# A state-space scan layer on eight cores: batched start statistics, five weight casts on another engine, a scan ring of four

## The reference, cut

```python
xn = layernorm(x)                                   # x: (1, 16384, 1024)
delta = softplus(einsum('btd,ed->bte', xn, Wd) + bd)
a_pos = softplus(a_log) + 0.0001                    # (1024, 16)
# for every token t, channel d and state n (16 states):
#   state = exp(-delta*a_pos)*state + delta*b_param*xn
# y = sum of the 16 states
attn = einsum('btd,ed->bte', y, Wo) + bo
real = einsum('bti,io->bto', xn, cos(theta + theta_noise))
imag = einsum('bti,io->bto', xn, sin(phi + phi_noise))
out  = x + attn + sqrt(real*real + imag*imag)
```

## Time and profile before

| | us |
|---|---|
| median of 2 runs | 1109.86 (1109.3 to 1110.43) |
| the profiled execution's own time | 1110.03 |
| its span on the slowest core (core 4) | 1108.2 |
| spans of the eight cores | 1099.7 to 1108.2 |
| first scan starts on core 4 | 71.09 |

### The profile page before, as it was taken

The page is one execution under the profiler, slowest core; times in us unless marked ns, Lnnn a source line. Parts: engine busy times, 40 slices in busy tenths (PEclk is TensorE's granted clock), DMA queues, the critical chain, the costliest instruction groups (busy, mean ns, idle before and its releaser), DMA issues.

```text
span 1108.2 us, 9244 instructions; the slowest of 8 cores (1099.7 to 1108.2 us)
## 1 busy us (share of the span) xinstructions
PE 572.1 (52%) x2239; PEld 240.3 (22%) x2248; DVE 816.4 (74%) x725; ACT 582.4 (53%) x927; POOL 150.4 (14%) x132
## 2 busy tenths in 40 slices
PE   0522444445457554556545456665555555454785
PEld 0300111112113231222211113343222211121343
DVE  3449888898853349999999993334899999999423
ACT  4485876666633226666665553332466655555430
POOL 2467000000011200000000001121000000000232
PEclk9985555556678866666665668887766556666799
DMA  8887101000011410000000001331100000000023
GB/s 235 208 224 195 57 29 29 29 19 1 0 48 57 122 37 0 1 1 0 1 1 1 0 0 48 88 114 58 43 1 1 0 1 1 1 0 1 29 72 114
DMA packets 36324, 51.65 MB, mean 47 GB/s; under 512 B 3120, under 2 KB 19760, under 8 KB 36272
## 3 DMA queue, kind: packets, MB, share of 16 engines
q1 hardware_dynamic: 33584, 42.68, 13.8%
q0 software_dynamic: 2688, 8.39, 2.3%
HBM read 42.67 MB, written 8.39 MB: 46 GB/s over the span
## 4 chain that ended last, share of the span: by engine, by line
DVE 46%; PE 17%; ACT 17%; issue 17%; DMA 2%; DVEq 1%; ACTq 0%; POOL 0%; SPq 0%; POOLq 0%
DVE grot L723 36%; ACT abar L677 9%; PE pd L852 6%; ACT bdg_bf L171 3%; PE pt L570 3%; PE pt L580 2%; DVE sfm L866 2%; DVE vbuf L333 2%; DMA xsub<-xin 2%; DVE gcar L734 1%; PE pd L278 1%; PE pe L357 1%; PE py L880 1%; DVE xsub L419 1%; PE pt L357 1%
## 5 line engine op out<-in xcount | busy, mean ns | idle before, releaser
L723 DVE TENSOR_TENSOR_SCAN grot<-abar,gcar,vbuf 128x768 bf16<-128x768 f32 (+1 forms) x384 | 647.0, 1742 | 41.1 <-ACT abar L677 32.4
L677 ACT ACTIVATE abar<-delta,nega 128x768 f32<-128x768 f32 (+1 forms) x384 | 341.2, 898 | 242.5 <-DVE grot L723 240.3
L767 PE MATMUL pe<-grot,bdg_bf 128*128 128x384 bf16 x256 | 86.6, 443 | 119.1 <-DVE grot L723 119.1
L767 PE MATMUL py<-grot,bdg_bf 128*128 128x384 bf16 x256 | 85.7, 441 | 119.7 <-DVE grot L723 119.6
L278 PE MATMUL pd<-xnbf,wd_bf 128*128 128x384 bf16 (+1 forms) x368 | 98.7, 450 | 18.1 <-ACT xsub L297 14.7
L754 PE MATMUL py<-grot,bdg_bf 128*128 128x512 bf16 x61 | 32.5, 544 | 78.9 <-DVE grot L723 78.5
L852 PE MATMUL pd<-ybf,wo_bf 128*128 128x384 bf16 (+1 forms) x318 | 72.4, 377 | 0.3 <-issue 0.2
L620 POOL TENSOR_TENSOR xsub<-r,i 128x384 f32<-128x384 f32 (+1 forms) x9 | 18.1, 2009 | 388.4 <-ACT i L612 388.4
L570 PE MATMUL pt<-xnbf,cos_bf 128*128 128x384 bf16 (+1 forms) x319 | 69.9, 367 | 0.2 <-issue 0.2
L754 PE MATMUL pe<-grot,bdg_bf 128*128 128x512 bf16 x63 | 33.7, 545 | 68.5 <-DVE grot L723 68.5
L278 PEld LDWEIGHTS pd<-xnbf,wd_bf 128*128 128x128 bf16 x368 | 49.6, 135 | 67.2 <-issue 58.9
(11 more groups left out here) (105 smaller groups left out, 559.3 us busy)
## 6 DMA issues: line engine op xcount, KB each, us to landing
xsub<-xin SPq DMA_DIRECT2D x14, 512.0 KB, 4.4
xres<-xin SPq DMA_DIRECT2D x32, 192.0 KB, 2.5
out<-osub POOLq DMA_DIRECT2D x32, 192.0 KB, 2.7
xres<-xin SPq DMA_DIRECT2D x8, 256.0 KB, 4.1
out<-osub POOLq DMA_DIRECT2D x8, 256.0 KB, 3.4
r<-wdt SPq DMA_DIRECT2D x6, 256.0 KB, 5.4
i<-wdt SPq DMA_DIRECT2D x6, 256.0 KB, 6.0
etmp<-tht SPq DMA_DIRECT2D x6, 256.0 KB, 4.9
```

The costliest lines, as they stand in the source:

```text
L677: sx = run("scalar", lambda e, sl=sl_ab, par=par, dt=dt, n=n, tp=tp: e.activation(out=abar[:, sl * TP:sl * TP + tp], in_=delta[:, par * TP ...
L723: vs = run("vector", lambda e, g=gsl, sl=sl_ab, par=par, dt=dt, n=n, tp=tp: e.tensor_tensor_scan(out=grot[:, g * TP:g * TP + tp], data0=ab ...
L767: td = run("tensor", lambda e, c=c, g=gsl, dt=dt, n=n, bb=ypair[c]: e.matmul(bb[:, 0:384], bdg_bf[:, (dt * NST + n) * P:(dt * NST + n + 1) ...
```

## The change

Three edits.

1. In stage A of phase 0 the five tiles get their own scratch columns (`bn6` grows to 12 columns a tile, `bnA` holds mean and variance of all, `lnv` has six columns). DVE does the statistics of all five tiles without waiting for ACT, and then one Ln, one Exp and one product handle all five.
2. The last five of the 16 Wd pieces (11 to 15) no longer use the staging slots and POOL. SP loads them into five idle places (`vbuf`, `osub`, `xres`) without a wait, and ACT casts them after stage A, ahead of the diagonals of blocks 2 to 5. The Wd product waits for both engines' casts.
3. The ring `grot` has four slots in place of five, and the carried columns are copied after n = 3, 7, 11 and 15, four at a time.

```diff
-        grot = sbuf("grot", [P, 5 * TP], BF16)
+        grot = sbuf("grot", [P, 4 * TP], BF16)
...
+        wds_slots = [vbuf[:, 0:512], vbuf[:, 512:1024], osub[:, 512:1024],
+                     xres[:, 0:512], xres[:, 512:1024]]
+        wds_sems = ["LX5", "LW0", "LW1", "LR", "LR1"]
...
             if kind == "cast":
+                piece = off // 512
+                if piece >= 11:
+                    q = piece - 11
+                    la = run("sync", lambda e, s=src0, q=q: e.dma_start(
+                        out=wds_slots[q], in_=s), wds_sems[q], 16)
+                    wd_s_jobs.append((q, la, dst, off))
+                    continue
                 sl = wslot_next()
...
-                for ts in range(NSUBL[0]):
+                nsub0 = NSUBL[0]
+                vag = 0
+                for ts in range(nsub0):
                     wait("vector", xsems[ts], lxev[ts])
-                    wait("vector", "V", prev_vts)
                     run("vector", lambda e, ts=ts, a=xslots[ts]: e.bn_stats(
-                        out=bn6[:, 0:6], in_=a[:, 0:512]), "V")
+                        out=bn6[:, ts * 12:ts * 12 + 6], in_=a[:, 0:512]), "V")
...
                     wait("vector", "V", vst)
-                    wait("vector", "S", prev_s1)
-                    vag = run("vector", lambda e: e.bn_aggr(out=bn2[:], in_=bn6[:]), "V")
...
+                    vag = run("vector", lambda e, ts=ts: e.bn_aggr(
+                        out=bnA[:, ts * 2:ts * 2 + 2],
+                        in_=bn6[:, ts * 12:ts * 12 + 12]), "V")
...
+                s1 = run("scalar", lambda e, a=var_ap, w=nsub0: e.activation(
+                    out=lnv[:, 0:w], in_=a, func=AF.Ln, bias=cvals[:, 1:2]), "S")
+                wait("scalar", "S", s1)
+                s2 = run("scalar", lambda e, w=nsub0: e.activation(
+                    out=rstd6[:, 0:w], in_=lnv[:, 0:w], func=AF.Exp,
+                    scale=-0.5), "S")
+                wait("vector", "S", s2)
+                v1 = run("vector", lambda e, a=mean_ap, w=nsub0: e.scalar_tensor_tensor(
+                    out=negmr6[:, 0:w], in0=a, scalar=cvals[:, 2:3],
+                    in1=rstd6[:, 0:w], op0=ALU.mult, op1=ALU.mult), "V")
...
                 emit_stage_a(0)
+                for (q_, la_, dst_, off_) in wd_s_jobs:
+                    wait("scalar", wds_sems[q_], la_)
+                    s_ev = run("scalar", lambda e, d=dst_, o=off_, q=q_: e.activation(
+                        out=d[:, o:o + 512], in_=wds_slots[q], func=AF.Copy), "S")
...
                 for dtq in range(2, 6):
                     bdg_ev[dtq] = ("S", emit_diag_s(dtq, 0, NST))
...
-                    gsl = n % 5
+                    gsl = n % 4
...
-                    if n in (4, 9, 14):
-                        g0 = n - 4
+                    if n % 4 == 3:
+                        g0 = n - 3
                         wait("vector", "V", vs)
-                        gs = grot[:].rearrange("q (s t) -> q s t", s=5)[:, :, tp - 1:tp]
+                        gs = grot[:].rearrange("q (s t) -> q s t", s=4)[:, :, tp - 1:tp]
                         vc = run("vector", lambda e, a=gs, dt=dt, g0=g0: e.tensor_copy(
-                            out=gcar[:, dt * NST + g0:dt * NST + g0 + 5], in_=a), "V")
...
-                    elif n == 15:
```

More of the change, by code:

```diff
@@ L80, in _build @@
         cvals = sbuf("cvals", [P, 3])
-        bn6 = sbuf("bn6", [P, 12])
+        bn6 = sbuf("bn6", [P, 12 * NSUB])
         bn2 = sbuf("bn2", [P, 2])
-        lnv = sbuf("lnv", [P, 1])
+        bnA = sbuf("bnA", [P, 2 * NSUB])
+        lnv = sbuf("lnv", [P, NSUB])
         rstd = sbuf("rstd", [P, 1])
@@ L241, in _build @@
         ev_abar_free = [0, 0, 0]
-        ev_g_free_t = [0, 0, 0, 0, 0]
-        ev_g_free_v = [("V", 0)] * 5
+        ev_g_free_t = [0, 0, 0, 0]
+        ev_g_free_v = [("V", 0)] * 4
         ev_sfm_free_t = [0, 0]
@@ L274, in emit_sp_mm @@
                 wait("tensor", "V", bfree_v.get(keys[c], 0))
-                wait("tensor", "G", grp_done[id(wd_bf)])
+                gdw = grp_done[id(wd_bf)]
+                if isinstance(gdw, list):
+                    for sm_, evv_ in gdw:
+                        wait("tensor", sm_, evv_)
+                else:
+                    wait("tensor", "G", gdw)
                 tmm = None
@@ L329, in emit_vmult @@
                 wait(eng, "T", ev_p0_slots.get(5, 0))
+            if p == 0 and dt < 2:
+                wait(eng, "S", ev_wds_s[0])
             for rj in (8, 9, 10):
@@ L404, in emit_a_subtile @@
             wait("vector", "S", prev_s1)
-            vag = run("vector", lambda e: e.bn_aggr(out=bn2[:], in_=bn6[:]), "V")
+            vag = run("vector", lambda e: e.bn_aggr(out=bn2[:], in_=bn6[:, 0:12]), "V")
             wait("scalar", "V", vag)
@@ L409, in emit_a_subtile @@
             s1 = run("scalar", lambda e: e.activation(
-                out=lnv[:], in_=bn2[:, 1:2], func=AF.Ln, bias=cvals[:, 1:2]), "S")
+                out=lnv[:, 0:1], in_=bn2[:, 1:2], func=AF.Ln, bias=cvals[:, 1:2]), "S")
             wait("scalar", "S", s1)
             s2 = run("scalar", lambda e: e.activation(
-                out=rstd[:], in_=lnv[:], func=AF.Exp, scale=-0.5), "S")
+                out=rstd[:], in_=lnv[:, 0:1], func=AF.Exp, scale=-0.5), "S")
             wait("vector", "S", s2)
@@ L441, in emit_stage_a @@
                     vst = run("vector", lambda e, ts=ts, a=xslots[ts]: e.bn_stats(
-                        out=bn6[:, 6:12], in_=a[:, 512:1024]), "V")
+                        out=bn6[:, ts * 12 + 6:ts * 12 + 12], in_=a[:, 512:1024]), "V")
                     wait("vector", "V", vst)
-                    wait("vector", "S", prev_s1)
-                    vag = run("vector", lambda e: e.bn_aggr(out=bn2[:], in_=bn6[:]), "V")
-                    wait("scalar", "V", vag)
-                    wait("scalar", "S", prev_s2)
@@ L448, in emit_stage_a @@
[L448 to L457, removed]
@@ L458, in emit_stage_a @@
-                    prev_vts, prev_s1, prev_s2 = v1, s1, s2
+                    vag = run("vector", lambda e, ts=ts: e.bn_aggr(
+                        out=bnA[:, ts * 2:ts * 2 + 2],
+                        in_=bn6[:, ts * 12:ts * 12 + 12]), "V")
+                var_ap = bnA[:].rearrange("q (s t) -> q s t", t=2)[:, 0:nsub0, 1:2]
+                mean_ap = bnA[:].rearrange("q (s t) -> q s t", t=2)[:, 0:nsub0, 0:1]
+                wait("scalar", "V", vag)
+                s1 = run("scalar", lambda e, a=var_ap, w=nsub0: e.activation(
+                    out=lnv[:, 0:w], in_=a, func=AF.Ln, bias=cvals[:, 1:2]), "S")
@@ L472, in emit_stage_a @@
                     par = ts % 2
+                    wait("vector", "V", v1)
+                    wait("vector", "S", s2)
                     vts = run("vector", lambda e, ts=ts, a=xslots[ts]: e.tensor_scalar(
@@ L506, in _build @@
                 emit_stage_a(0)
+                for (q_, la_, dst_, off_) in wd_s_jobs:
+                    wait("scalar", wds_sems[q_], la_)
+                    s_ev = run("scalar", lambda e, d=dst_, o=off_, q=q_: e.activation(
+                        out=d[:, o:o + 512], in_=wds_slots[q], func=AF.Copy), "S")
+                    ev_wds_s[0] = s_ev
+                    if q_ == 3:
+                        ev_xres_free2[0] = ("S", s_ev)
+                    elif q_ == 4:
+                        ev_xres_free2[1] = ("S", s_ev)
+                grp_done[id(wd_bf)] = [("G", grp_done[id(wd_bf)]),
+                                       ("S", ev_wds_s[0])]
+                ev_init_s = max(ev_init_s, ev_wds_s[0])
                 for dtq in range(2, 6):
@@ L729, in _build @@
                     ev_abar_free[sl_ab] = vs
-                    if n in (4, 9, 14):
-                        g0 = n - 4
+                    if n % 4 == 3:
+                        g0 = n - 3
                         wait("vector", "V", vs)
-                        gs = grot[:].rearrange("q (s t) -> q s t", s=5)[:, :, tp - 1:tp]
+                        gs = grot[:].rearrange("q (s t) -> q s t", s=4)[:, :, tp - 1:tp]
                         vc = run("vector", lambda e, a=gs, dt=dt, g0=g0: e.tensor_copy(
-                            out=gcar[:, dt * NST + g0:dt * NST + g0 + 5], in_=a), "V")
-                        for s5 in range(5):
-                            ev_g_free_v[s5] = ("V", vc)
-                    elif n == 15:
[L739 to L743, removed]
+                            out=gcar[:, dt * NST + g0:dt * NST + g0 + 4], in_=a), "V")
+                        for s4 in range(4):
+                            ev_g_free_v[s4] = ("V", vc)
                     if n == 7 and dt + 1 < NDT:
@@ L834, in _build @@
                 lrs = "LR" if xrs == 0 else "LR1"
-                wait("sync", "V", ev_xres_free2[xrs])
+                wait("sync", ev_xres_free2[xrs][0], ev_xres_free2[xrs][1])
                 lr = run("sync", lambda e, t0=tok0, dt=dt, w=wdth, xrs=xrs: e.dma_start(
```

9 lines of the change are left out of this document (6 added, 3 removed).

## The result

| | before | changed |
|---|---|---|
| median, us | 1110.66 (12 runs) | 1105.1 (13 runs) |
| ratio, changed to before | | 0.9946 (95% interval 0.9932 to 0.996) |
| span of the profiled execution | 1108.2 | 1102.9 |

A run is now and then disturbed; the ratio leaves such runs out. By it the change gains 6.0 us (4.4 to 7.5), well inside 2%. The time, 1105.1, lies in the forecast range of 1100 to 1112; the forecast gain was 3.6 us.

What follows compares the result with a forecast made beforehand. DVE's scans, end to end in phases 1 and 2, and a serial start before the first scan were taken as the bounds. 1110.0 - 4.2 (start) + 0.6 (ring) = 1106.4 us; own range 1103 to 1109.5, stated range 1100 to 1112.

Steps and rivals of the forecast that it cites:

- The statistics: Stage A: without the waits for ACT, the first normalisation moves from 27.40 to 18.7 us, -8.7 us.
- The rest of stage A: Normalisations, transposes and copies behind the first normalisation: unchanged, so ACT's last bf16 copy moves as much.
- The casts: Five casts on ACT between the last bf16 copy and the diagonals, on the path: +2.8 us.
- What POOL takes back: Block 0, scans beside POOL's adds: 2.0 us lost, 0.3 regained, so 4.2 of 5.9 us kept.
- the lower bound: Start: 3.0 us kept if each of 2.3 more adds beside scans blocks for its whole 1.26 us.
- the sign of the forecast: Start of block 1: at 108.4 us, against 112.6 before, would show the forecast loss to POOL.
- The ring's copies: Copies between scans: 0.19 us saved a block in about eight undisturbed blocks, with others -2 us in all.
- The ring's waits: Scan n = 4 waits for PE's product of n = 0 in five blocks: +2.6 us.
- The 1.3 us of block 6: Block 6, scan n = 4: a wait of 1.3 us for PE, counted in full as lost time.
- (a): Start keeps nothing, as POOL's adds end when they end and block 0 with them: 1110 to 1111 us, chance 0.13.
- (b): Ring stalls scan n = 4 in 13 FFN blocks: over 1110, about 1143 us at full price; chance 0.11.
- (c): Start keeps more, POOL ahead by 3.1 us, copies save their full 4 us: 1102 down to 1099, chance 0.15.

Runs made afterwards that it cites:

- e5: The kernel before with POOL's 32 adds of weight pairs cut from 512 to 16 columns (thin adds); 1094.61 us, one run.
- e9: The changed kernel itself, run again in the same rounds as e10; 1102.62 us, ratio 0.9942.
- e4: The changed kernel without the five casts on ACT, all 16 Wd casts on POOL again; 1102.51 us, ratio 0.9948 to the kernel before.
- e10: The same kernel as e4, run again beside the changed kernel; 1102.41 us, ratio 0.9935.
- e8: e4 with the diagonals of blocks 3 to 7 built by ACT within blocks 0 to 5, not ahead of softplus; 1096.14 us, ratio 0.9853.
- e7: The changed kernel with one wait more: scan n also waits for PE's product of n - 3; 1136.65 us, ratio 1.0228.
- e1: The kernel before with the batched statistics alone; 1103.24 us, ratio 0.9947.
- e6: The changed kernel with POOL's adds cut from 512 to 16 columns (thin adds); 1091.13 us, one run.

## Why the prediction was right, and where its sizes were off

**The statistics.** Forecast -8.7 us at the first normalisation, measured -9.1 on the mean of the cores. Right, by the steps given: landings at the pace of the transfers, 1.6 us a tile, an unchanged tail.

**The rest of stage A.** Taken as unchanged, it was 0.7 us shorter on the mean of the cores (from the first normalisation to the last bf16 copy, 20.1 and 19.5 us). Before, the last two normalisations met POOL's adds, which had begun by then (timeline of POOL and DVE before):

```profile
35.95 1.26 POOL L220 TENSOR_TENSOR cos_bf<-etmp 128x512 bf16<-128x512 f32 x1 [2.93 <-DMA etmp<-thn]
...
38.61 1.74 DVE L473 TENSOR_SCALAR abar<-abar,rstd,negmr 128x1024 f32<-128x1024 f32 x1
...
43.15 1.30 DVE L473 TENSOR_SCALAR sfm<-sfm,rstd,negmr 128x1024 f32<-128x1024 f32 x1
```

After, the first of these two starts at 29.55 and takes 0.80 us (above), and the first add comes later than that:

```profile
34.21 1.26 POOL L233 TENSOR_TENSOR cos_bf<-etmp,r 128x512 bf16<-128x512 f32 x1 [6.40 <-DMA r<-thn]
```

The step that failed is "the normalisations, transposes and copies behind it are unchanged": work that moves earlier can also leave a stage in which POOL stretched it. The thin kernel before (e5) shows that it is the adds: there the last three normalisations take 0.80 us each without having moved, and the same stretch is 19.0 us.

**The casts.** Forecast +2.8 us, measured +2.6 on the mean of the cores (the diagonals start 2.5 us behind the end of the last bf16 copy, at 40.3 and 37.8, where before they started 0.1 us ahead of it). The cover stood: softplus followed the diagonals.

**What POOL takes back.** Forecast a loss of 1.7 of 5.9 us. Measured: 1.9 of 7.3 between the first scan and the end of phase 0, or about 2.5 without the ring's 0.6 there; 2.9 of 10.9 with edit 1 alone. Over all pairs (e9, e4, e10 and e8 against e4 too) it is 21 to 34 per cent, about what was forecast, and the thin adds show that it is POOL. The two factors of the forecast were off in opposite ways. Forecast were 2.3 more adds beside scans at 0.88 us; on the mean of the cores 16.6 adds ended after the first scan's start before and 19.9 after, so 3.3 more at about 0.76 us. In the other pairs an add cost 0.66 to 0.73 us, and only 0.48 from e4 to e8 (6.1 more adds). None comes near the whole 1.26 us of the lower bound; why an add cost less than the forecast 0.88 stays open.

The place was half right: block 0 kept its length and the loss came up in block 1, 2.9 us on the mean of the cores, as the adds that remain there. So block 1 started at 104.0 us, not at the 108.4 that was named as the sign of the forecast. That POOL would be ahead by 1 us is not resolved: the last add ended at 111.2 us on the mean of the cores in one execution and at 108.5 in the other (e9), against 110.3 before.

**The ring's copies.** By the steps from scan to scan, the copy ahead of the vbuf product costs 0.28 us and the others 0.46, in the changed kernel as computed; undisturbed blocks (2, 4, 5, 13 and 21) got 0.20 to 0.21 us shorter (forecast 0.19), FFN blocks without a wait 0.05 (forecast: nothing). The price of a copy is right. The sum is not quite: the last blocks of the phases have no vbuf product behind n = 7, so nothing was saved there, and blocks 15 and 23 got 0.15 us longer, block 7 0.2 to 0.5. Over all blocks that makes about 1 us instead of 2.

**The ring's waits.** Forecast +2.6 us in five blocks. In phases 1 and 2 they were where forecast, at n = 4 of blocks 10, 11, 19 and 20, and sometimes 14: 1.3 us on the mean of the cores, and 1.2 in e9, against 1.3. (Before had 0.4 us of its own, at n = 5 of block 18.) The 1.3 us of block 6 are the term that was wrong. The wait came, 0.8 us on the mean of the cores, and cost nothing. The timeline of the changed kernel:

```profile
258.01 4.43 DVE L760 TENSOR_TENSOR_SCAN grot<-abar,gcar,vbuf 128x640 bf16<-128x640 f32 x3 [0.94 <-PE py L785]
263.54 1.55 DVE L760 TENSOR_TENSOR_SCAN grot<-abar,gcar,vbuf 128x640 bf16<-128x640 f32 x1 [1.09 <-ACT abar L714]
```

and the same wait for ACT before:

```profile
271.13 1.55 DVE L723 TENSOR_TENSOR_SCAN grot<-abar,gcar,vbuf 128x640 bf16<-128x640 f32 x1 [1.93 <-ACT abar L677]
```

Three scans later DVE waits for ACT in any case (two table loads and four Sin stand in ACT's order there), and the wait for ACT shrinks by what the wait for PE took. The prediction asked what a stall hides behind for the edits it costed at nothing, but not for this one.

It hides only because of where it stands. In block 6 of e7 the wait for PE comes one scan earlier, at n = 3, and there it costs its full length, 2.8 us on the mean of the cores in a block that is 2.9 us longer (timeline of DVE, core 3):

```profile
259.84 1.55 DVE L762 TENSOR_TENSOR_SCAN grot<-abar,gcar,vbuf 128x640 bf16<-128x640 f32 x1 [3.34 <-PE py L787]
...
268.12 1.55 DVE L762 TENSOR_TENSOR_SCAN grot<-abar,gcar,vbuf 128x640 bf16<-128x640 f32 x1 [1.92 <-ACT abar L714]
```

The wait for ACT at n = 7 is as long as before, 1.9 us. ACT's last abar ahead of the table loads is that of n = 6, and with three slots it needs the end of scan n = 3. A wait behind that scan finds ACT already on its way; a wait ahead of it makes ACT late as well.

**The sum.** Forecast: 4.2 us kept from the start, less 0.6 for the ring. Measured on the mean of the cores: 5.4 us at the end of phase 0, of which the thin kernels give 0.6 to the ring, so 4.8 from the start; and 0.4 us lost in phases 1 and 2, so that the ring comes out at +0.2 us gained. The terms that were mis-sized are the shift of the first scan (7.3 us instead of 5.9), the copies and block 6. That the last two nearly cancel, about 1 us too much saved by the copies and 1.3 us too much lost in block 6, is luck. The 5.0 us of this sum lie in the measured interval of 4.4 to 7.5; the last microsecond to 6.0 isn't resolved. The other execution of the changed kernel (e9) gives 6.5 us by the same reading, while the spans of before and changed differ by 4.4 us on the mean of the cores. The prediction took 22 us for about what a measurement can tell from no change; the interval here is 3.1 us wide.

**The rivals.** (a), nothing kept, falls with e1, e6 and e8. (b), the ring stalling the scans, is real as a mechanism, and e7 shows its price at a higher dose, but at four slots it is 1.3 us. (c), more than forecast, is the side on which the time lies, though not for its reasons: POOL was 0.9 us behind in one execution of the changed kernel and 1.7 us ahead in the other, not 3.1, and the copies saved less than forecast, not more.

## What to carry to other kernels

A saving ahead of a stage in which two engines block each other is paid back in part there; the share can be read before the change, as the stage's excess over a free one, divided by the blocking instructions and their pitch. Here that reading gives 0.88 / 2.53, 35 per cent, and the runs lost 21 to 34, so it is an upper estimate. Before work is moved onto the engine that sets a stage's end, look at whether the wait that it relieves was the one that came last: five casts went onto ACT's path to free a product that lay under 18.9 us of cover, while the cover itself was what could be moved, for another 9 us (0.9853 against 0.9935 of the kernel before, in the same rounds). And a new wait can cost nothing when another wait stands behind it, but only if it doesn't delay the engine that the second wait is for: in block 6 the wait for PE was free at n = 4 and cost its whole length at n = 3.

## What the runs showed of the hardware

A scan of 640 columns takes 1.55 us alone and 2.5 beside POOL's adds; when the adds read 16 columns instead of 512, block 0 runs at its free pace, although an add of 16 columns was then itself held for up to 1.27 us against 0.22 undisturbed. So the length of the add and not its mere presence sets the price. That fits what the Trainium skill says (page SBUF — State Buffer, section SBUF: two separate sides), that whichever starts first holds the shared port for the whole instruction. The price itself was lower than a whole add: 0.5 to 0.8 us for each further add beside the scans, where an add alone takes 1.26 us.

The mean granted clock of the span was 0.659 to 0.686 on the eight cores with the extra wait of e7, against 0.695 to 0.708 in the changed kernel. In the ten blocks that wait, the clock in the Wd and FFN products was 0.70 instead of 0.75, PE came to the products of n = 0 later, and the waits cost a fifth more than the rows of before had said (22.6 us against 18 to 19). That the wait lowered the clock is not shown: four of the cores had 0.81 to 0.83 instead of 0.95 to 0.96 in the last stage too, where nothing was changed.
